# Decoder layer on one core: experts' tables by small matrix products, routing moved up, merges spread over six chunks

## The reference, cut to what matters

```python
x = _layernorm(x + _L0_attn_ref(...)); x = _layernorm(x + _L0_xattn_ref(...))
scores = softmax(xf @ Wg.T); expert_weights, expert_indices = top_k(scores, 2)
h1, h3 = (einsum('td,ehd->teh', xf, W) + low rank (A, B) + b for W1, W3)
y_e = lora_out(silu(h1) * h3, W2, b2, A2, B2)
y = sum over the two chosen experts of weight * y_e;  x = _layernorm(x + y)
```

## Time and profile before

| | us |
|---|---|
| median of 3 runs (lowest, highest) | 1417.0 (1416.65, 1417.9) |
| the profiled execution, its own time | 1421.66 |
| its span | 1419.9 |
| PE, DVE, ACT, POOL busy | 1321.8, 868.2, 831.3, 715.8 |

### The profile page before, as it was taken

One profiled execution on the slowest core, in us unless ns is written; L12 is line 12 of the kernel. 1 busy time (PEld: TensorE's weight loads), 2 busy tenths in 40 slices (PEclk: granted clock), 3 DMA queues, 4 the chain that ended last, 5 costly groups with the idle time before them and its releaser, 6 DMA issues. The chain is left out here.

```text
span 1419.9 us, 19346 instructions
## 1 busy us (share of the span) xinstructions
PE 1321.8 (93%) x6367; PEld 581.8 (41%) x6367; DVE 868.2 (61%) x1410; ACT 831.3 (59%) x1011; POOL 715.8 (50%) x507
## 2 busy tenths in 40 slices
PE   8988999999999999996999999659999999999966
PEld 3443222222222222222344544426666666666645
DVE  3443788888888888884168785734444444444426
ACT  4544899999999999994655555112222222222237
POOL 2232677777777777773255877422333333333313
PEclk9998899999999999998799998779999999999988
DMA  6598444495557444524344445611111111111147
GB/s 221 159 334 259 174 69 68 82 253 81 81 130 181 68 68 81 92 48 135 107 133 125 142 143 175 201 62 41 46 45 49 45 47 48 45 42 48 42 142 232
DMA packets 108043, 161.31 MB, mean 114 GB/s; under 512 B 29457, under 2 KB 69302, under 8 KB 107638
## 3 DMA queue, kind: packets, MB, share of 16 engines
q1 hardware_dynamic: 97936, 132.87, 36.6%
q0 software_dynamic: 9888, 27.08, 5.8%
q10 hardware_dynamic: 118, 0.05, 0.0%
HBM read 111.96 MB, written 48.27 MB: 113 GB/s over the span
## 5 line engine op out<-in xcount | busy, mean ns | idle before, releaser
L676 DVE TENSOR_TENSOR sa_probs<-sa_sum,sa_strips 128x1024 f32<-128x1024 f32 x352 | 413.1, 1218 | 74.3 <-PE sa_sum L631 70.0
L718 POOL TENSOR_TENSOR sa_probs<-sa_probs,sa_factors 128x1024 f32<-128x1024 f32 x160 | 381.0, 2381 | 134.3 <-ACT sa_probs L694 134.3
L700 ACT ACTIVATE sa_probs<-sa_probs 128x1024 f32<-128x1024 f32 (+1 forms) x256 | 341.2, 1374 | 0.3 <-DVE sa_probs L676 0.3
L645 PE MATMUL sa_o<-sa_probs,sa_v 128*17 128x512 f32 x2048 | 270.3, 600 | 1.1 <-POOL sa_probs L718 0.6
L2217 PE MATMUL xp_ps_h<-big,arena 128*128 x568 | 257.9, 597 | 1.2 <-ACT arena L2268 1.1
L631 PE MATMUL sa_sum<-sa_q,sa_k 97*128 97x512 bf16 x704 | 199.2, 387 | 6.2 <-PEq L134 4.4
L2268 ACT ACTIVATE arena<-xp_ps_x 128x256 f32<-128x256 f32 x71 | 27.2, 383 | 296.1 <-PE xp_ps_x L2209 296.1
L2190 POOL DMA_INDIRECT y_places<-stage,xp_place_of x71 | 69.8, 983 | 255.0 <-DVE stage L2319 255.0
L694 ACT ACTIVATE sa_probs<-sa_factor 128x1024 f32<-128x1024 f32 x160 | 163.2, 1020 | 29.0 <-PE sa_factor L631 29.0
L2217 PEld LDWEIGHTS xp_ps_h<-big,arena 128*128 128x128 f32 x568 | 108.6, 192 | 108.9 <-issue 105.4
L631 PEld LDWEIGHTS sa_sum<-sa_q,sa_k 97*128 97x128 bf16 x704 | 48.5, 98 | 251.2 <-DVE sa_probs L676 195.2
(11 more groups left out here) (234 smaller groups left out, 1469.3 us busy)
## 6 DMA issues: line engine op xcount, KB each, us to landing
sa_q<-qstack SPq DMA_DIRECT2D x96, 128.0 KB
sa_k<-kstack SPq DMA_DIRECT2D x96, 128.0 KB
sa_strips<-line SPq DMA_DIRECT2D x3, 3840.0 KB, 16.5
oT<-sa_o_out SPq DMA_DIRECT2D x32, 256.0 KB, 2.3
co_y<-y_places SPq DMA_DIRECT2D x16, 512.0 KB, 8.9
kstack<-qp_parts SPq DMA_DIRECT2D x48, 128.0 KB, 3.7
qstack<-qp_parts SPq DMA_DIRECT2D x48, 128.0 KB
sa_factors<-factor_line SPq DMA_DIRECT2D x3, 1920.0 KB, 20.6
```

What stands on the lines that cost most here:

```text
L645: last = nc.tensor.matmul(ps_o[n % 2][32 * h:32 * h + VW, :], v[m % 2][:, jt, VW * h:VW * (h + 1)], probs[s % RING][:, h, :], start=(jt == ...
L676: nc.vector.tensor_tensor(probs[s % RING][:, 2 * half:2 * half + 2, :], ps_sum[sums_before(s, half) % 2][:, :, :], strips[hg % 2][:, 2 * h ...
L700: nc.scalar.activation(probs[s % RING][:, 0:heads, :], probs[s % RING][:, 0:heads, :], ACT.Exp, scale=0.25).then_inc(exp_done, 1)
L718: nc.gpsimd.tensor_tensor(probs[s % RING][:, 2:4, :], probs[s % RING][:, 2:4, :], factors[hg % 2][:, :, c1 - CH:c1][:, :, ::-1], ALU.mult) ...
```

## The change

1. **Opening.** The even units of `low_rank` are copied by ACT, the odd ones by DVE (`copy_low` on both engines). `turn_x1(0)` comes after six units instead of ten, and eight units follow the queries instead of four. POOL makes the root of chunk 0 before it scales chunk 1.
2. **Merges.** The sixteen merges lie in iterations 0 to 5 (two, then three in each of 1 to 4, then two) instead of two in each of 0 to 7. The added one stands between the second `add_projection` and the moments. SP's loads are moved to match, and the biases are loaded earlier.
3. **Routing of chunk 6.** DVE chooses it before the divisions of chunk 7 and places it between them, PE ranks it between the turned tiles, and POOL scatters two of its tiles before `root2(7)`.
4. **W2.** The units alternate between both PSUM buffers; units 0, 1 and 6 are added by DVE. Two come before `turn_x2(7)`.
5. **Tables.** The counts are taken on eight partitions, one for each expert; one small product sums them, DVE forms five numbers for each expert and tile (8 x 355), and a product with ones spreads them over 128 partitions. The weights' last three steps move into `experts`.

The core of the diff:

```diff
-W2_BANK = (0, 1, 1, 1, 1, 1, 1, 0)
-W2_ADDED = (0, 6, 7)
+W2_ADDED = (0, 1, 6)
+W2_COPIED = (2, 3, 4, 5, 7)
...
 def count(nc, ro, ps):
-    return nc.tensor.matmul(ps[:, TT * RANKS:TT * RANKS + RANKS], ro["ones"][:, :], ro["before"][:, NTT, :],
-                            start=True, stop=True)
+    first, all_rows = ps[0:E_, TT * RANKS:TT * RANKS + 1], ps[0:E_, TT * RANKS + 1:TT * RANKS + 2]
+    one = ro["ones"][:, 0:1]
+    nc.tensor.matmul(first, ro["before"][:, NTT, 0:E_], one, start=True, stop=True)
+    nc.tensor.matmul(all_rows, ro["before"][:, NTT, 0:E_], one, start=True, stop=False)
+    return nc.tensor.matmul(all_rows, ro["before"][:, NTT, E_:RANKS], one, start=False, stop=True)
+def sum_tiles(nc, ro, ps):
+    return nc.tensor.matmul(ps[0:E_, 0:1], ro["tri8"][:, :], ro["columns"][:, 2:3], start=True, stop=True)
+def spread_tables(nc, ro, ones, ps, chosen_jumps):
+    return nc.tensor.matmul(ps[:, 0:5 * NT], ones[0:E_, :], chosen_jumps.rearrange("p q s -> p (q s)"), start=True, stop=True)
...
-def tabulate(nc, release, step, ro, ps, scratch):
+def count_tiles(nc, release, step, ro, ps):
+    columns, count_i = ro["columns"], ro["count_i"]
+    release(nc.vector.tensor_copy(columns[:, 0:2], ps[0:E_, TT * RANKS:TT * RANKS + 2]))
+    step(nc.vector.tensor_scalar(count_i[:, 0:1], columns[:, 1:2], float(P - 1), None, ALU.add))
+    step(nc.vector.tensor_scalar(count_i[:, 1:2], count_i[:, 0:1], 7, None, ALU.arith_shift_right))
+    return nc.vector.tensor_copy(columns[:, 2:3], count_i[:, 1:2])
+def find_jumps(nc, step, ro, ps, chosen_jumps):
+    columns, jumps, select = ro["columns"], ro["jumps"], ro["select"]
+    first, every, tiles, end, start, begin = (columns[:, n:n + 1] for n in range(6))
+    step(nc.vector.tensor_copy(end, ps[0:E_, 0:1]))
+    step(nc.vector.tensor_tensor(start, end, tiles, ALU.subtract))
+    nc.vector.tensor_scalar(select[:, 0, :], ro["slots"][:, :], end, None, ALU.is_ge)
+    step(nc.vector.tensor_scalar(begin, start, float(P), None, ALU.mult))
+    step(nc.vector.scalar_tensor_tensor(out=select[:, 1, :], in0=ro["slots"][:, :], scalar=start, in1=select[:, 0, :],
+                                        op0=ALU.is_ge, op1=ALU.subtract))
+    nc.vector.tensor_tensor(jumps[:, 0:1], ro["region8"][:, 0:1], start, ALU.subtract)
+    nc.vector.tensor_tensor(jumps[:, 1:2], begin, first, ALU.add)
+    nc.vector.tensor_tensor(jumps[:, 2:3], begin, every, ALU.add)
+    nc.vector.tensor_scalar(jumps[:, 3:4], first, -1.0, float(T), ALU.mult, ALU.add)
+    step(nc.vector.tensor_copy(jumps[:, 4:5], ro["region8"][:, 1:2]))
+    return nc.vector.tensor_tensor(chosen_jumps, select[:, 1, :].unsqueeze(1).to_broadcast([E_, 5, NT]),
+                                   jumps[:, :].unsqueeze(2).to_broadcast([E_, 5, NT]), ALU.mult)
+def tabulate(nc, step, ro, ps, scratch):
     space = CrossSpace(scratch)
...
-    for n in range(4):
-        step(nc.vector.tensor_tensor(part, passed, gaps[:, n, :].unsqueeze(1).to_broadcast([P, NT, E_ - 1]), ALU.mult))
-        step(nc.vector.tensor_reduce(sums[n], part, AXX, ALU.add))
...
+    second, valid, jump, row = (space.take(P, NT) for _ in range(4))
+    number, dummy = ro["number"], ro["dummy"]
+    start, bound, end, skip, owner = (ps[:, n * NT:(n + 1) * NT] for n in range(5))
+    nc.vector.tensor_tensor(second, number[:, :], bound, ALU.is_ge)
+    nc.vector.tensor_tensor(valid, number[:, :], end, ALU.is_lt)
+    step(nc.vector.scalar_tensor_tensor(out=row, in0=start, scalar=float(P), in1=number[:, :], op0=ALU.mult, op1=ALU.add))
+    step(nc.vector.tensor_tensor(jump, second, skip, ALU.mult))
+    step(nc.vector.tensor_tensor(row, row, jump, ALU.add))
+    step(nc.vector.tensor_tensor(row, row, dummy[:, :], ALU.subtract))
+    step(nc.vector.tensor_tensor(row, row, valid, ALU.mult))
+    nc.vector.tensor_copy(ro["tile_expert"][:, :], owner[0:1, :])
+    step(nc.vector.tensor_tensor(ro["row_of"][:, :], row, dummy[:, :], ALU.add))
+    return nc.vector.scalar_tensor_tensor(out=ro["choice_at"][:, :], in0=second, scalar=float(T), in1=valid, op0=ALU.mult,
+                                          op1=ALU.mult)
...
                 load_outputs(sp, io, oc[n % 2], recb[n % 2], n, o_loaded[n % 2])
+                if n >= 3:
+                    load_piece(3 * (n - 3) + 1)
                 sp.wait_ge(kept, TT * (n - 1))
                 sp.wait_ge(masked, TT * (n - 1))
                 load_residual(sp, io, x1[n % 2], n, x_loaded[n % 2])
                 if n >= 3:
-                    load_piece(2 * n - 4)
-                load_piece(2 * n - 3)
+                    load_piece(3 * (n - 3) + 2)
+                    load_piece(3 * (n - 3) + 3)
...
-            sp.dma_start(f2, io["factors2"].rearrange("q p c -> p q c")).then_inc(f2_loaded, 16)
-            load_piece(12)
-            load_piece(13)
+            sp.dma_start(f2, io["factors2"].rearrange("q p c -> p q c")).then_inc(factors_loaded, 16)
             wait_filled(sp, "project", NCH - 1, 1)
             sp.wait_ge(scaled, NCH)
+            load_bias(0)
+            load_bias(1)
             sp.wait_ge(kept, TT * NCH)
             sp.wait_ge(masked, TT * NCH)
+            load_bias(2)
             wait_filled(sp, "q", NCH - 1, KT - 1)
-            load_piece(14)
-            for e in range(5):
-                load_bias(e)
-            load_piece(15)
+            load_bias(3)
+            load_bias(4)
...
-                    pe.wait_ge(exp_done, u - 1)
+                    pe.wait_ge(low_done if u % 2 else exp_done, u // 2)
...
+            def tables():
+                pe.wait_ge(ro["counted"], 1)
+                for i in range(2):
+                    pe.wait_ge(att_drained[i], NCH * (ATT // 2))
+                sum_tiles(nc, ro, ps_att[0]).then_inc(att_filled, 1)
+                pe.wait_ge(ro["counted"], 2)
+                spread_tables(nc, ro, ones, ps_att[1], chosen_jumps).then_inc(att_filled, 1)
...
-            for u in range(10):
+            for u in range(6):
                 low_rank(u)
             turn_x1(0)
-            low_rank(10)
-            low_rank(11)
+            low_rank(6)
+            low_rank(7)
             queries(0)
-            for u in range(12, LOW):
+            for u in range(8, LOW):
...
+                if n + 1 == NCH:
+                    ranks(NCH - 2)
...
             low_rank2(0)
+            low_rank2(1)
             turn_x2(NCH - 1)
-            ranks(NCH - 2)
             gate(NCH - 1)
-            low_rank2(1)
-            ranks(NCH - 1)
-            for u in range(2, 8):
-                low_rank2(u)
             pe.wait_ge(verdict, 1)
             wait_bank(pe, "verdict", NCH, 0)
             nc.tensor.matmul(bank("verdict", NCH, 0)[:, 0:2], ones[:, :], good[:, :],
                              start=True, stop=True).then_inc(misc_filled, 1)
+            low_rank2(2)
+            ranks(NCH - 1)
+            low_rank2(3)
+            tables()
+            for u in range(4, 8):
+                low_rank2(u)
...
-            for u in range(10):
+            for u in (0, 2, 4):
                 copy_low(u)
             copy_x1(0)
-            copy_low(10)
-            copy_low(11)
+            copy_low(6)
             copy_queries(0)
-            for u in range(12, LOW):
+            for u in range(8, LOW, 2):
...
             copy_x2(NCH - 1)
-            copy_w2(1)
-            for u in range(2, 8):
-                if u not in W2_ADDED:
-                    copy_w2(u)
+            copy_w2(2)
             act.wait_ge(weighed, 1)
...
+            for u in W2_COPIED[1:]:
+                copy_w2(u)
...
-                tabulate(nc, release, step, ro, bank("rank", NCH - 1, 0), scratch)
+                ps = bank("rank", NCH - 1, 0)
+                count_tiles(nc, step, step, ro, ps).then_inc(ro["counted"], 1)
+                dve.wait_ge(ro["counted"], 1)
+                dve.wait_ge(att_filled, ATT * NCH + 1)
+                find_jumps(nc, step, ro, ps_att[0], chosen_jumps).then_inc(ro["counted"], 1)
+                dve.wait_ge(att_filled, ATT * NCH + 2)
+                step(tabulate(nc, step, ro, ps_att[1], scratch))
+            def copy_low(u):
+                w, k, q, i = low_pairs()[u]
+                dve.wait_ge(l_filled, u + 1)
+                nc.vector.tensor_copy(w13[w][:, 4 * q + 2 * i:4 * q + 2 * i + 2, k, :], ps_l[1][:, :, :]).then_inc(low_done, 1)
...
             add_projection(0, 0)
             add_projection(0, 1)
             moments1(0, statistics1(0))
+            copy_low(1)
+            copy_low(3)
             normalise_masked(0)
+            for u in range(5, LOW, 2):
+                copy_low(u)
             dve.wait_ge(cc["den_loaded"], 16 * B)
...
                     divide(n - 1, (0, 1))
                     if n >= 2:
                         choose_experts(n - 2)
-                    merge()
+                    if n <= 5:
+                        merge()
                     divide(n - 1, (2, 3))
```

(31 more changed lines are left out.)

178 lines of the change are left out of this document (74 added, 104 removed).

## The result

The changed kernel took **1441.1 us** (median of 4 runs, 1434.8 to 1444.5) beside 1417.45 us (4 runs, 1416.65 to 1422.7) for the kernel before: a ratio of **1.0136, 95% interval 1.0108 to 1.0165**. It is slower; the forecast of 1413.7 and the whole range were wrong. The profiled execution took 1438.66 us, its span 1436.1, where the one before had 1421.66 and 1419.9. The profiles so lie 17.0 us apart and the medians 23.7; what follows accounts for the profiles, and where the other 6.7 us of the medians lie no profile shows. A second chip gave 1.0104 (1.0062 to 1.0146) for the same kernel.

A forecast was written before the change was run, and what follows sets the result against it. PE and DVE were taken to run locked together in the middle chunks, with one chain at the end. 0.4 + 5.4 - 0.9 - 3.4 - 4.8 = -3.3 us, from 1417.0 to 1413.7; range 1408.5 to 1420.5.

The forecast's parts named there:

- Merges, iterations 1 to 5: Middle chunks: the added merge on DVE delays PE's turning and POOL's steps; +5.4 us (+1.0 to +8.0).
- The slower rival: Iterations 1 to 5: merges, pieces and POOL hold each other up, 12 us instead of 5.4, 1420.3 in all; chance 0.18.
- Iteration 6 and the turning of chunk 6: Iteration 6: first merge and most of the 1.19 gap gone, -0.9; iteration 7: 2.80 gap gone, chunk 7 turned earlier, -3.4.
- The end: From the turning of chunk 7 to the block's end: shorter tables, W2 ending last with two buffers; -4.8 us.
- the end gains little: Tables: PE's wait of about 2 us lowers the clock, two W2 units cost 4.5 us, 1418.2 in all; chance 0.17.
- The opening: Before the first scores: copies halved on ACT, DVE's passes added; +0.4 us (-2.0 to +2.5).

The follow-up runs named there:

- e8: Changed kernel with fifteen of the sixteen piece loads left out, every merge adding the first piece again; its six periods took 148.5 us.
- e5: Changed kernel with the end merge's piece loaded ahead of the outputs and the middle merge moved behind `normalise2`; six periods 153.6 us.
- e3: Changed kernel with `take_gates` moved ahead of the merge at the iteration's end; 1443.0 us.
- g1: Changed kernel with old opening, merges 0 to 13 at old places, two in the end, a W2 unit between the tables' products; 1414.2 us, ratio 0.9938.
- g3: As g1, but without the unit of W2 between the tables' products; ratio 0.9967 to the kernel before.
- e4: Changed kernel with the load of the end merge's piece put ahead of the four loads of the next outputs; 1444.2 us.
- e7: Changed kernel with both edits of e5 and a unit of W2 between the tables' two products; six periods 153.4 us.
- e2: Kernel before with only the merges and their loads of the changed kernel; 1450.4 us beside 1433.9 for the kernel before.
- e6: Changed kernel with one unit of W2 moved on PE between the tables' two products; 32.4 us from chunk 7's turning to ACT's last W2 copy.
- h1: As g1 but with the changed kernel's opening, and `normalise_masked(0)` moved ahead of DVE's copy of product 3; ratio 0.9948.

## Why the prediction was wrong

The forecast was -3.3 us, and the profiles gave +17.0. Of the 20 us between them, 12.7 lie in the six periods, 3.9 in the end, 2.0 from chunk 7's projection to its turning, and 0.5 in the opening.

- **Merges, iterations 1 to 5: +5.4, the step that failed.** The six periods measured +18.1. The term was built from the merge's time on DVE, and e8 measures that at +5.9: right. What it gave to late pieces in the middle chunks was "0.4 a chunk" at its upper end and nothing in the sum; with the pieces' loads go 12.3 us, some 2 a chunk with the clock behind the gaps. The order of SP's loads was read ("SP's loads stand in one line"), but not priced with the landing time of a piece behind four transfers (9.5 us), and nothing was asked about what stands *behind* the end merge: `take_gates`, and PE's bank behind it. The gap in chunk 1 of the kernel before, 4.91 us for a piece, was the warning, and was treated as a case of that chunk.
- **The slower rival (0.18)** named the single `stage` buffer and late pieces, and priced them at 12 us for merges and pieces together; 18.1 was measured for the six periods. Its place was off, the end merge behind the outputs' loads instead of the next chunk's first merge; that one became the bottleneck in e5, and DVE held by POOL's `scale` in e3.
- **Iteration 6 and the turning of chunk 6: -0.9 and -3.4, measured -2.3.** The 1.19 us gap and the 2.80 us gap are gone, and the turning of chunk 6 is at the upper clock (1.09): the mechanism was right. The two halves of chunk 7's projection stand 3.01 us apart instead of 4.27, which is -1.3 where -0.9 was forecast. From there to the turning of chunk 7 only 1.0 of the 3.4 us came: PE's wait for DVE's choice of chunk 6, which the forecast had in its sum (3.9 us, "PE waits for it"), is a new gap of 3.16 us, and the clock is low behind it, which the sum did not have. In g1 and g3, which keep merges in iteration 6, C is 54.8 and 55.9 us; the windows show a clock of 0.75 from 860 to 870 us in g1 and of 0.60 from 870 to 880 us in g3. Why it fell there was not followed up.
- **The end: -4.8, measured -0.9.** The rival "the end gains little" came true for the reason it gave: a gap of 2.24 us in the tables (2 was its estimate) and units at the lower clock. With the gap filled the end gains 7.6 (34.5 to 27.0), more than the 4.8: what the sum lacked was the clock behind the gap in the tables.
- **The opening: +0.4 (to +2.5)**, measured +0.9 in A by the first profiles, and 6.4 and 9.9 by the medians of the two pairs that differ in it: outside its range, with the cause open in part. The sum had the copies' time (1.22, as measured) but not that two of them on DVE push its normalisation beside POOL's `scale(1)`. The part of the edit on POOL, `scale(1)` behind `root1(0)`, was not costed, and no run undoes it alone. The Trainium skill ("SBUF — State Buffer", section "SBUF: two separate sides") gives the exclusive lock for DVE with two SBUF inputs, and for DVE in a 2-port mode; the forecast applied only the first half, to the merges. The trace agrees that these `tensor_scalar` operations, which have one large input, are held too, in seven profiles; no row tells in which mode they run.

Of the marks that were to show it, the scores started at 699.79 (698 to 701, right). The periods were 3.0 us longer instead of about 1, and merges of the middle chunks waited 2.0 to 2.7 us for pieces, where none beyond 1 was expected. Chunk 7 was turned at 916.16 (900.3 was forecast), and the block ended at 949.8 (anything after 935 was said to prove the forecast wrong). The gather came 5.7 us behind the block's end (6.3).

## What to carry to other kernels

When work behind a DMA is moved or made denser, price three things besides its own time: how long its transfer takes from its place in the queue of loads, what stands behind the waiting instruction on its engine, and which buffer that one frees. An operation of 0.18 us behind a late piece cost PE 2.9. A gap of about 2 us on PE can cost more than its length: behind the 2.24 us in the tables the units ran at 1.2 GHz, and a piece of independent PE work placed in it paid 7 us by the profiles and 3 by the medians (the ratios' intervals overlap). Late work is best put where the engine already waits for something else: two merges in such waits cost at most 0.6 us.

## What the chip showed unexpectedly

- DVE is held until a large POOL operation ends, also for short ones and for `tensor_scalar`: four normalisations of 1.37 us took 3.50, a merge of 1.22 took 3.37 and, in e4 and e7, a comparison of 0.19 took 1.91, beside a POOL product of 2.34 us.
- The four gaps of 1.7 to 2.9 us in the middle chunks of the changed kernel were each followed by the lower clock (0.50 to 0.61 in the 4 us behind them). Not every gap of that length is: in g3 gaps of 1.90 and 1.78 us before the second half of a projection, and in e3 of 1.98 and 1.91 us, were followed by a clock of 1.00. PE, then the windows, in g3:

```profile
796.60 1.56 PE L1192 MATMUL cb_misc<-arena,big 128*128 128x256 f32 x6 [1.90 <-DVE big L1502]
```

```profile
796.60:801.00 4.40, 4.40 (x32) 2.08 (x32) 4.26 (x18) 1.59 (x3) 2.10 (x4) 1.00 0.51 167
821.20:826.00 4.80, 4.79 (x32) 2.08 (x32) 4.54 (x19) 2.11 (x3) 2.42 (x4) 1.00 0.69 203
```

- Spells at the lower clock also came without a gap: in g1 the clock was 0.50 from 760 to 763 us and the queries of chunk 3 took 4.86 us, while PE's timeline shows no gap from 749 us on. What starts those stays open.
- In e2, e6, e7, h1 and the control of the kernel before, ACT began the copy of a unit of W2 some 2 to 6 us after PE's records say that it was full. The trace names no releaser, but in each case the semaphore that PE raises at the end of the unit rises 0.02 to 0.03 us before the copy (at 924.15 for the copy at 924.17, in the control): the signal was late, not ACT. Why stays open. D of the two profiles of the kernel before differs by 8 us, 6 of them this stall.
